# GpSimd splits layer 0's weights, TensorE multiplies identities in its early gaps, and the prologue of a three-layer graph transformer is put in another order

## The reference, cut to what matters

```python
h = relu(layernorm(x))                       # x: 64 graphs x 128 nodes x 256
for l in range(3):
    si = h @ attn_w[l, :256];  sj = h @ attn_w[l, 256:]
    scores = leaky_relu(si[:, :, None] + sj[:, None, :] + attn_b[l], 0.2)
    attn = softmax(where(adj | eye, scores, -inf))
    agg = attn @ h
    h = layernorm(h + agg) * g1[l] + beta1[l]
    ff = gelu(h @ W1[l] + b1[l]) @ W2[l] + b2[l]      # 256 -> 1024 -> 256
    h = layernorm(h + ff) * g2[l] + beta2[l]
out = x + h
```

## Time and profile before

| what | value |
|---|---|
| median of three runs | 1233.32 us |
| profiled execution, its own time | 1233.53 us |
| span of its trace | 1231.7 us |
| TensorE matmuls busy | 1190.9 us, 97% |
| VectorE busy | 1058.8 us, 86% |
| ScalarE busy | 988.7 us, 80% |
| GpSimd busy | 677.0 us, 55% |

### The profile page before, as it was taken

One profiled execution on the slowest core, in us unless ns is written; L12 is line 12 of the kernel. 1 busy time (PEld: TensorE's weight loads), 2 busy tenths in 40 slices (PEclk: granted clock), 3 DMA queues, 4 the chain that ended last, 5 costly groups with the idle time before them and its releaser, 6 DMA issues.

```text
span 1231.7 us, 23195 instructions
## 1 busy us (share of the span) xinstructions
PE 1190.9 (97%) x7325; PEld 1086.1 (88%) x7325; DVE 1058.8 (86%) x3483; ACT 988.7 (80%) x1944; POOL 677.0 (55%) x648
## 2 busy tenths in 40 slices
PE   2799999999999999999999999999999999999997
PEld 1698999999899999999999999999999999999996
DVE  7889888899998888889998888889999888888754
ACT  5777888789888887888888778878888788788853
POOL 2326544556675455546765555455657554645474
PEclk9799999999999999999999999999999999999999
DMA  7243233235432322244344222233454222222322
GB/s 235 62 144 87 78 117 87 73 95 154 147 112 81 102 76 61 85 115 123 116 129 128 87 61 86 88 86 87 126 156 134 83 86 86 69 61 91 116 70 69
DMA packets 142744, 124.73 MB, mean 101 GB/s; under 512 B 16632, under 2 KB 123164, under 8 KB 142620
## 3 DMA queue, kind: packets, MB, share of 16 engines
q1 hardware_dynamic: 142620, 123.23, 33.6%
HBM read 78.53 MB, written 44.66 MB: 100 GB/s over the span
## 4 chain that ended last, share of the span: by engine, by line
PE 92%; DVE 4%; ACT 1%; POOL 1%; issue 1%; DMA 0%; SPq 0%; DVEq 0%; POOLq 0%
PE acc L1164 43%; PE hbank L1149 41%; PE mix L1181 7%; DVE junk L768 0%; DVE xs L836 0%; DVE hid_lo L667 0%; DMA adji<-in_adj_dram 0%; DVE st L843 0%; ACT xs L1061 0%; POOL rstd L511 0%; DVE xs L849 0%; DVE junk L777 0%; DVE sc L804 0%; DVE st L655 0%; POOL hb L538 0%
## 5 line engine op out<-in xcount | busy, mean ns | idle before, releaser
L1164 PE MATMUL acc<-w2hi,hid_hi 128*128 128x256 f32 x1536 | 443.5, 289 | 1.3 <-DVE hid_lo L667 1.3
L1164 PE MATMUL acc<-w2hi,hid_lo 128*128 128x256 f32 x1536 | 434.9, 283 | 0.0
L1164 PE MATMUL acc<-w2lo,hid_hi 128*128 128x256 f32 x1536 | 434.7, 283 | 0.0
L994 ACT ACTIVATE hbank<-hbank,vec 128x512 f32<-128x512 f32 x384 | 254.4, 662 | 139.6 <-PE hbank L1149 133.8
L1149 PE MATMUL hbank<-ht_hi,w1hi 128*128 128x512 f32 x768 | 303.2, 395 | 4.7 <-DVE hid_lo L667 3.7
L1164 PEld LDWEIGHTS acc<-w2hi,hid_hi 128*128 128x128 f32 x1536 | 294.6, 192 | 12.8 <-DVE hid_lo L667 2.4
L1164 PEld LDWEIGHTS acc<-w2lo,hid_hi 128*128 128x128 f32 x1536 | 293.9, 191 | 10.4
L1149 PE MATMUL hbank<-ht_lo,w1hi 128*128 128x512 f32 x768 | 302.4, 394 | 0.0
L1149 PE MATMUL hbank<-ht_hi,w1lo 128*128 128x512 f32 x768 | 299.4, 390 | 0.0
L667 DVE TENSOR_TENSOR hid_lo<-hbank,hid_hi 128x512 fp32r<-128x512 f32 x384 | 258.9, 675 | 41.5 <-ACT hid_hi L1000 41.1
L1164 PEld LDWEIGHTS acc<-w2hi,hid_lo 128*128 128x128 f32 x1536 | 293.8, 191 | 0.0
(11 more groups left out here) (91 smaller groups left out, 1777.7 us busy)
## 6 DMA issues: line engine op xcount, KB each, us to landing
z_dram<-tz SPq DMA_DIRECT2D x46, 512.0 KB, 2.6
zt<-z_dram SPq DMA_DIRECT2D x184, 128.0 KB, 3.0
sj_bc<-sj_dram SPq DMA_DIRECT2D x47, 256.0 KB, 3.6
e_dram<-te SPq DMA_DIRECT2D x46, 256.0 KB, 2.0
ET<-e_dram SPq DMA_DIRECT2D x184, 64.0 KB, 2.1
out_dram<-xout SPq DMA_DIRECT2D x32, 256.0 KB, 4.0
xraw<-in_x_dram SPq DMA_DIRECT2D x15, 512.0 KB, 5.1
xres<-in_x_dram SPq DMA_DIRECT2D x15, 512.0 KB, 4.3
```

Source lines behind the costliest of these rows:

```text
L994: act.activation(hbank[k % HB][:], hbank[k % HB][:], ACT.Gelu, bias=b1c(i.l, c)).then_inc(gelu_n, 1)
L1164: mm = pe.matmul(to, v[:, k % HID, of_g], w[:, i.l, c], start=c == 0 and n == 0 and g % HG == 0, stop=c == C - 1 and n == 2, skip_group_ch ...
```

## The change

1. Halves 0 to 3 of the weights (layer 0) are split by GpSimd and no longer by VectorE. VectorE keeps halves 4 to 11; its `split_weights` has one wait more, so that the two engines count `w_lo` in order.
2. For item 0, `z1_turn` writes its two transposes into the two banks `acc` and not into `util`, with no wait for `util`; `h_high` and `h_low` read them there.
3. `keep_warm(n)` issues n matmuls of the 128x128 fp32 identity by itself into a bank `hbank` that nobody reads yet: 20 ahead of `sj_rows` of item 0, 32 ahead of `e_turn` of item 0, 20 ahead of `e_turn` of item 1, and 6 ahead of `z1_turn` of item 0.
4. The prologue's order is another one on all five engines. From slot 1 on, nothing is changed.

```diff
+        def turned_in(q, m):
+            if q == 0:
+                return acc[m][:].rearrange("p g d -> p (g d)")
+            return util[:]
...
+            def split_weights(n):
+                pool.wait_ge(w_hi, n + 1)
+                pool.tensor_tensor(half_on_chip(1, *halves[n]), half_staged(n),
+                                   half_on_chip(0, *halves[n]).bitcast(F32), ALU.subtract).then_inc(w_lo, 1)
...
             make_rstd("0", i1.g)
+            bias_rows()
+            split_weights(0)
             make_rstd("0", i2.g)
-            bias_rows()
+            split_weights(1)
+            split_weights(2)
             make_rstd("1", i0.q)
             h_gamma(i0, 0)
+            split_weights(3)
             h_gamma(i0, 1)
+            make_rstd("0", i3.g)
             h_beta(i0, 0)
-            make_rstd("0", i3.g)
             make_rstd("1", i1.q)
+            h_gamma(i1, 0)
+            h_gamma(i1, 1)
             h_beta(i0, 1)
-            h_gamma(i1, 0)
+            h_beta(i1, 0)
             make_rstd("1", i2.q)
-            h_gamma(i1, 1)
             h_gamma(i2, 0)
-            h_beta(i1, 0)
...
+            def keep_warm(n):
+                for _ in range(n):
+                    pe.matmul(hbank[HB - 1][:, 0:P], ident[:], ident[:], start=True, stop=True)
...
+            keep_warm(20)
             sj_rows(i0)
+            keep_warm(32)
             e_turn(i0)
             aggregate(i0, 0)
             aggregate(i0, 1)
+            keep_warm(20)
             e_turn(i1)
+            keep_warm(6)
             z1_turn(i0, 0)
+            z1_turn(i0, 1)
             aggregate(i1, 0)
-            aggregate(i1, 1)
-            z1_turn(i0, 1)
```

More of the change, by code:

```diff
@@ L917, in _ @@
             turn_vectors()
+            input_shift(i0)
             penalty(i0)
-            input_shift(i0)
-            penalty(i1)
             j_dots(i0)
@@ L925, in _ @@
             masked(i0)
-            split_weights(0)
+            penalty(i1)
+            j_dots(i1)
             minus_max(i0)
-            j_dots(i1)
-            split_weights(1)
-            split_weights(2)
             input_moments(i2)
             i_dots(i1)
+            penalty(i2)
             attend(i0, 0)
-            input_shift(i2)
             masked(i1)
@@ L938, in _ @@
             moments1(i0)
+            input_shift(i2)
+            penalty(i3)
+            norm1(i0)
             j_dots(i2)
-            penalty(i2)
-            norm1(i0)
+            h_low(i0, 0)
+            h_low(i0, 1)
             input_moments(i3)
-            h_low(i0, 0)
+            i_dots(i2)
+            low(i0, 0)
+            masked(i2)
             attend(i1, 0)
-            masked(i2)
-            h_low(i0, 1)
+            input_shift(i3)
+            low(i0, 1)
+            minus_max(i2)
+            low(i0, 2)
             attend(i1, 1)
-            i_dots(i2)
+            low(i0, 3)
             moments1(i1)
[L950 to L954, removed]
+            turn_e(i2)
+            split_weights(4)
             norm1(i1)
-            turn_e(i2)
-            low(i0, 1)
-            split_weights(4)
+            low(i0, 4)
             j_dots(i3)
[L960 to L963, removed]
             low(i0, 5)
-            h_low(i1, 0)
             i_dots(i3)
             low(i0, 6)
+            h_low(i1, 0)
+            low(i0, 7)
+            split_weights(5)
             attend(i2, 0)
+            h_low(i1, 1)
             masked(i3)
             attend(i2, 1)
-            h_low(i1, 1)
+            minus_max(i3)
             moments1(i2)
-            minus_max(i3)
-            low(i0, 7)
+            residual(i0, 0)
+            residual(i0, 1)
             low(i1, 0)
             norm1(i2)
-            residual(i0, 0)
-            residual(i0, 1)
             for s in range(1, ITEMS + 3):
@@ L1022, in h_high @@
                 wait(act, ffn1_n, C * (i.q - 1))
-                act.copy(ht_hi[:, i.q % 2, m], util[:]).then_inc(hthi_n, 1)
+                act.copy(ht_hi[:, i.q % 2, m], turned_in(i.q, m)).then_inc(hthi_n, 1)
             def norm2(i, h):
@@ L1126, in _ @@
             gelu_high(i1, 1)
-            round_weights(6)
             exps(i3)
@@ L1205, in z1_turn @@
                     pe.wait_ge(z1_n, GG * i.q + g + 1)
-                    mm = pe.transpose(util[:, g * P:(g + 1) * P], x_of(i)[:, g, m * P:(m + 1) * P], ident[:])
+                    mm = pe.transpose(t[:, g * P:(g + 1) * P], x_of(i)[:, g, m * P:(m + 1) * P], ident[:])
                 mm.then_inc(zt_n, 1)
@@ L1256, in _ @@
             ffn1(i0, 2)
+            aggregate(i1, 1)
             ffn1(i0, 3)
             ffn2(i0, 0)
-            z1_turn(i1, 0)
             ffn2(i0, 1)
             ffn1(i0, 4)
+            ffn2(i0, 2)
             ffn1(i0, 5)
             ffn1(i0, 6)
-            ffn2(i0, 2)
             ffn2(i0, 3)
+            z1_turn(i1, 0)
+            ffn2(i0, 4)
             ffn1(i0, 7)
+            ffn2(i0, 5)
             aggregate(i2, 0)
+            z1_turn(i1, 1)
             aggregate(i2, 1)
-            z1_turn(i1, 1)
-            ffn2(i0, 4)
-            ffn2(i0, 5)
+            ffn2(i0, 6)
+            ffn2(i0, 7)
             ffn1(i1, 0)
             ffn1(i1, 1)
-            ffn2(i0, 6)
-            ffn2(i0, 7)
             ffn1(i1, 2)
```

46 lines of the change are left out of this document (25 added, 21 removed).

## The result

The changed kernel took 1236.72 us (median of 13 runs, 1234.90 to 1237.69) against 1233.38 us for the kernel before beside it (13 runs): a ratio of 1.0025, 95% interval 1.0018 to 1.0032. It is slower by 3.3 us. The profiled execution took 1236.99 us, its span is 1235.2 us. Two executions of a later kernel, e12, took 1307.71 and 6565.58 us, were in a slow state, and are left out of its median and its ratio.

The account below looks back on a forecast made before the run. VectorE, which TensorE waits for, was taken as the bound. Item 2's turn_z 2.9 us late, less slot 1's 0.1 to 0.3, gave 1233.53 + 2.7 = 1236.2, less 0.2 for the median: 1236.0 us; range 1226.0 to 1238.0.

Parts of the forecast that it names:

- VectorE sets the time, through `turn_z`: Prologue: the time follows VectorE's start of item 2's turn_z, 2.9 us late, less 0.1 to 0.3 in slot 1.
- The price of a subtraction on GpSimd: Splitting layer 0's weights on GpSimd: 2.35 us for each 1024-column half, 9.4 us for four.
- the walk: Step-by-step sum of VectorE's prologue up to item 2's turn_z, with 8.6 us held by GpSimd.
- (a): Prologue to the end of item 1's masked: 30.5 us against 28.1, 2.4 late, with GpSimd's subtractions holding VectorE.
- (b): On to the end of item 0's second h_low: 42.9 us against 42.2, with j_dots of item 2 held twice.
- (c): On to item 0's first low: 46.9 us against 49.0, 2.1 early, with 4.9 us of work still owed.
- (d): On to item 2's turn_z: 26.5 us of work plus holds and idle gives 80.3, call by call 80.0, against 77.03.
- TensorE's waits for `low`: Sign to look for between 78 and 98 us: TensorE waits for low 2 to 4 us in all.
- Identity products: TensorE's added matmuls in the prologue: 0.18 us each, 52 done by 19 us, costed at nothing.
- Rival 1: Prologue: the engines hold each other little, turn_z at 70.8 to 71.5, 1227.3 us; chance 0.35.
- rival 2: Prologue: half the holding falls into VectorE's waits for ScalarE and rows, turn_z about 77, 1231 to 1235.8 us; chance 0.2.

Follow-up runs that it names:

- e12: e2 with sj of item 1 sent and loaded ahead of item 3's rows and adjacency: 1232.56 us.
- e4: The changed kernel without its 78 identity products: 1237.20 us.
- e2: The changed kernel with GpSimd setting layer 0's four low halves to zero instead of subtracting: 1233.01 us.
- e3: The changed kernel with two h_beta products on GpSimd moved away from j_dots of item 3: 1234.14 us.
- e1: The changed kernel with halves 0 to 3 split by VectorE again, in the new order: 1233.48 us.
- e6: The changed kernel with splits on VectorE, two h_beta products moved, and sj of item 1 sent and loaded ahead of item 3's loads: 1232.02 us.

## Why the prediction was right

It forecast 1236.0 us, slower by 2.7; measured was 1236.7, slower by 3.3. By its steps:

- **VectorE sets the time, through `turn_z`.** Right: the table above. The 0.1 to 0.3 us that slot 1 was to give back were 0.5 by the rest column (1154.7 and 1154.2), which is less than two profiles can tell.
- **The price of a subtraction on GpSimd**, 2.35 us: 2.36, 2.76, 2.40 and 2.40, at 20.3, 24.2, 26.9 and 37.2. The second stood 0.4 us behind a step of VectorE; that GpSimd can be the one held was not in the walk.
- **(a)** `masked` of item 1 ends at 30.5: it ended there (30.5), and by the way forecast: `i_dots` was held for 0.7 us (0.8 in the walk), `penalty`'s bf16 step until 27.1, and `masked` until 29.5 by the third subtraction. One part differs and didn't count, because the subtraction held longer: the rows of sj landed at 28.2, not 26.7. SyncE issued the transfer of item 1's result at 18.55, behind item 3's loads, which were in at 24.2, and asked for its rows at 24.40.
- **(b)** Second `h_low` of item 0 ends at 42.9: 43.1. `j_dots` of item 2 was held for 3.2 us, 3.4 in the walk.
- **(c)** First `low` ends at 46.9: 47.6. Of the 0.7 us, 0.2 come from (b) and 0.47 are a wait for ScalarE, the term that the walk put at nothing here.
- **(d)** `turn_z` at 80.0: 80.96. Most of the gap was there at the first `low`: from there it took 33.3 us, 33.1 in the walk. `j_dots` of item 3 was held for 2.9 us (2.5 in the walk), the waits for ScalarE came to 1.9 (0.44, 0.86 and 0.64, until 51.6, 54.0 and 57.0; 1.7 in the walk), and `masked` of item 2 waited 0.5 (0.8). What was sized too small in all is VectorE's wait for ScalarE, 2.4 us with (c)'s. The first chunks at half clock are a likely reason: in e4, where the first had the full clock at its start, these waits are 0.65 us in all, the one for sj is 0.6 longer, and turn_z is at 79.99.
- **TensorE's waits for `low`** between 78 and 98: 0.24, 1.05 and 1.54 us, 2.8 in all, 2 to 4 forecast. One of 1.8 us, until 66.96, was not forecast.
- **Identity products** of 0.18 us: 0.23 at 2.4 GHz (32 in 7.31). The first 20 took 6.60 at two paces, 20 records in the 4.0 us from 7 to 11 and 23 in the 2.3 us to 13.3; the view prints 1.00 for both, as it does ahead of its first record of the clock. At a granted 1.2 GHz the last six of e2 took 0.46 each:

```profile
33.02 2.77 PE L1152 MATMUL hbank<-ident 128*128 128x128 f32 x12
...
33.10:35.70 2.60, 2.60 (x14) 2.60 (x14) 1.67 (x5) 2.54 (x5) 1.66 (x2) 0.50 0.01 3
```

  The 52 ended at 21.1 and not at 19. The cover was there: VectorE read item 0's aggregate at 27.24 without a wait. Item 0's first chunks ran at half clock, as forecast, but not for the reason given, so this was luck: the pause from 39 to 42.3 was to bring it, and the clock had fallen by 34.8, after TensorE had stood from 29.4 to 32.6. It was at 0.50 from there to 47.9. In e2 and e3 it fell between 32 and 34 and was full again by 37.
- **Rival 1** ("the two engines hold each other little", chance 0.35, 1227.3 us) did not come: the engines held each other wherever the walk said. Its price was not tried. e2 took 1233.0, but it only takes away most of the holding by the splits. Of the 8.6 us held in the walk about 6.9 were still there (1.1 in `j_dots` of item 2, 2.0 in two `norm1`, 2.9 in `j_dots` of item 3, 1.0 in the wait of `masked` of item 2), and by its own rule the prediction wanted under 3.4. One of its steps is shown to be wrong: `masked` of item 1 was to end at 28.0 and ended at 29.6 in e2, because the rows of sj came at 28.1 and not at 26.7. With the splits' move alone nothing better than 1233 was seen.
- **Holding falls into VectorE's waits** (rival 2): partly so. In e2 the relief went there; in the changed kernel the holding was a loss.

**The rule on the shared ports.** The trace of before had no bf16 step beside a GpSimd operation: all 16 take 0.29 us. This one has: 2.32 us while a subtraction ran. The Trainium skill, "SBUF — State Buffer", section "Who interferes with whom", lists `tensor_scalar` among the operations that can take the shared pair of ports, and says that the engine that comes second then blocks for the whole instruction. The trace agrees. The same section says that an operation of VectorE with two SBUF inputs contends with a GpSimd instruction that reads SBUF and not with one that only writes it. The traces agree in one pair: VectorE's two-input step (L803) began 0.1 us ahead of a GpSimd operation in both, and the subtraction behind it took 0.4 us longer than the others (24.21 in the changed kernel), the memset its usual 0.95 (23.14 in e2). A two-input step that had to begin behind a memset is in no row. The bf16 step at 23.74 in e2 stood until the second memset ended at 24.98.

## What to carry to other kernels

Before work is moved from VectorE to GpSimd, write down what VectorE runs beside each of its operations: an operation of half a microsecond with two SBUF inputs stood here until a 2.4 us one ended, and a queue of three GpSimd operations took three of its instructions with it. So put GpSimd's work beside what VectorE reads from PSUM (`low` took its usual 0.69 at 46.94, beside a GpSimd product from 46.52 to 47.79) or beside its `BATCH_NORM_STATS2` (1.41 at 20.00, beside a subtraction from 20.29). One input is not enough: the `TENSOR_SCALAR` steps of `penalty` and `norm1` have one and were held. Price the relief too: work that fills an engine's pauses costs little where it stands (e1, where splits 2 and 3 run while the rows land), and taking it away gains only what the next transfer allows. Where an engine sets the time through one late moment, follow that moment across all variants: from it on, the profiled executions of fourteen kernels took 1154.0 to 1156.3 us.

## What the runs showed of the hardware that was not expected

- VectorE's bf16 `TENSOR_SCALAR` (128x512) was held by an operation of GpSimd that only writes: 1.38 us in place of 0.29 in e2. A two-input step that had begun just ahead of such an operation took its usual 0.69, and delayed it by nothing.
- A 2 KB transfer to DRAM sent at 18.2 landed at 24.1 in e2, behind 768 KB asked for earlier, and one sent at 18.3 at 22.1 in e12 without them; the load of 256 KB that follows took 3.8 to 5.3 us, the longer with three loads right behind it. Asking 2.0 us earlier gained 1.3 us in e12, and 1.7 us earlier gained 0.2 in e6.
- Holding goes both ways: a subtraction of GpSimd issued 0.13 us behind a two-input step of VectorE took 2.76 us in the changed kernel, the other three 2.36 to 2.40.
- A 128x128 product in fp32, two records, is 0.23 us at 2.4 GHz and 0.46 at 1.2 (six in 2.77, e2 and e3).
